# Other turns of the last tiles among three DRAM sums, and VectorE as the reporter of closed sums

## The reference

```python
x = x + tanh(g_xattn) * xattn(ctx, ctx, layernorm(x), ssm_kernel, D, 8)   # long convolution, 16 heads of 8
h = layernorm(x)                                                        # 2048 tokens x 256
s = sigmoid(h @ w_router); combine = s of the 6 chosen of 32 experts    # grouped top-k with a bias
routed = sum over the chosen e: combine[e] * (silu(h @ gate_w[e]) * (h @ up_w[e])) @ down_w[e]   # 256 -> 176 -> 256
shared = silu(h @ sh_gate_w) * (h @ sh_up_w) @ sh_down_w
out = x + tanh(g_ffn) * (routed + shared)
```

## Time and profile before

| | |
|---|---|
| median of 3 runs | 513.12 us |
| the profiled execution | 514.59 us, of which its span 512.8 us |
| PE busy | 435.5 us (85%) |
| POOL busy | 275.5 us (54%) |
| DMA at the two last slices of 40 | 9 and 9 tenths busy, 331 and 334 GB/s |
| PE clock granted there | 5 tenths of full speed; 9 or more in the slices before |

### The profile page before, as it was taken

One profiled execution on the slowest core, in us unless ns is written; L12 is line 12 of the kernel. 1 busy time (PEld: TensorE's weight loads), 2 busy tenths in 40 slices (PEclk: granted clock), 3 DMA queues, 4 the chain that ended last, 5 costly groups with the idle time before them and its releaser, 6 DMA issues.

```text
span 512.8 us, 8791 instructions
## 1 busy us (share of the span) xinstructions
PE 435.5 (85%) x2162; PEld 330.4 (64%) x2162; DVE 303.5 (59%) x1162; ACT 201.7 (39%) x522; POOL 275.5 (54%) x226
## 2 busy tenths in 40 slices
PE   0936989999999687799999999999999999999600
PEld 0726768768767565477777777777777777777400
DVE  4999898998986665334444444444444444444156
ACT  4531734644642511134444444444444444444300
POOL 2000027748758737558766666666566666666700
PEclk9986999999999698789999999999999999999955
DMA  6999913323369876858767666667666666666599
GB/s 257 383 354 396 384 40 130 130 75 107 120 214 366 299 262 201 256 195 133 127 118 127 113 114 116 118 114 125 114 112 115 116 123 119 116 115 103 67 331 334
DMA packets 59462, 91.56 MB, mean 179 GB/s; under 512 B 6797, under 2 KB 50189, under 8 KB 59149
## 3 DMA queue, kind: packets, MB, share of 16 engines
q1 hardware_dynamic: 35759, 55.07, 31.9%
q0 software_dynamic: 20160, 29.11, 31.6%
q10 hardware_dynamic: 3486, 6.73, 3.9%
HBM read 47.87 MB, written 43.02 MB: 177 GB/s over the span
## 4 chain that ended last, share of the span: by engine, by line
PE 69%; DVE 16%; DMA 7%; ACT 4%; issue 3%; DVEq 0%; SPq 0%; POOL 0%; POOLq 0%; ACTq 0%
PE bank L1261 24%; PE bank L1280 18%; PE bank L1250 5%; PE bank L1271 4%; DVE arena L702 4%; PE bank L1123 4%; PE bank L1103 3%; PE bank L1144 3%; PE bank L1091 3%; DMA arena<-token_sums 2%; DMA token_sums<-shd_sb,dest 2%; DMA payload<-expert_lists 2%; PE bank L1092 1%; ACT payload L548 1%; DVE arena L659 1%
## 5 line engine op out<-in xcount | busy, mean ns | idle before, releaser
L430 POOL DMA_INDIRECT expert_lists<-payload,slots x96 | 103.5, 1078 | 116.2 <-DVE slots L809 77.8
L1261 PE MATMUL bank<-wgu,work 128*128 x432 | 148.1, 466 | 1.3 <-DVE work L1018 1.3
L1280 PE MATMUL bank<-wd,work 88*128 x432 | 111.9, 382 | 0.0
L1036 DVE TENSOR_TENSOR work<-work,bank 128x176 f32<-128x176 f32 x108 | 36.5, 338 | 121.8 <-ACT work L593 121.8
L1261 PEld LDWEIGHTS bank<-wgu,work 128*128 128x128 f32 x432 | 74.8, 193 | 25.4 <-issue 2.9
L593 ACT ACTIVATE work<-bank 128x176 f32<-128x176 f32 x108 | 34.2, 317 | 111.4 <-PE bank L1261 111.4
L1280 PEld LDWEIGHTS bank<-wd,work 88*128 88x128 f32 x432 | 73.9, 191 | 6.2 <-issue 0.2
L445 POOL DMA_INDIRECT token_sums<-shgu_sb,dest x35 | 54.5, 1558 | 29.8 <-ACT shgu_sb L608 25.5
L1018 DVE COPY work<-bank 128x256 f32<-128x256 f32 x108 | 45.8, 424 | 28.9 <-PE bank L1250 28.9
L445 POOL DMA_INDIRECT token_sums<-q_sb,dest x28 | 43.6, 1558 | 23.6 <-ACT q_sb L608 15.9
L702 DVE TENSOR_TENSOR arena<-arena,q_sb 128x448 f32<-128x448 f32 (+7 forms) x120 | 45.4, 456 | 1.7 <-ACT arena L496 1.6
(11 more groups left out here) (174 smaller groups left out, 569.5 us busy)
## 6 DMA issues: line engine op xcount, KB each, us to landing
payload<-expert_lists SPq DMA_DIRECT2D x108, 152.0 KB, 2.6
wgu<-w_gu SPq DMA_DIRECT2D x9, 704.0 KB
expert_lists<-blank SPq DMA_DIRECT2D x1, 5016.0 KB, 23.4
wgu<-w_gu SPq DMA_DIRECT2D x1, 4928.0 KB, 18.9
arena<-token_sums SPq DMA_DIRECT2D x9, 512.0 KB, 8.8
wd<-w_down SPq DMA_DIRECT2D x4, 704.0 KB
token_sums<-blank SPq DMA_DIRECT2D x1, 2304.0 KB, 26.6
token_sums<-blank SPq DMA_DIRECT2D x1, 2176.0 KB, 23.0
```

What stands on the lines that cost most here:

```text
L430: nc.gpsimd.indirect_dma_start(lists, bass.IndirectOffsetOnAxis(ap=slots[:, g % 2, b, k:k + 1], axis=0), pay[g % 2][:, b, :], None).then_i ...
L1036: nc.vector.tensor_tensor(win(work, H_AT + t % 2 * M, [[1, M]]), win(work, SG_AT + t % 2 * M, [[1, M]]), bank[2 + t % 2][:, M:2 * M], ALU. ...
L1261: last = nc.tensor.matmul(bank[2 + t % 2][:, 0:2 * M], xT_half(t, k), wgu[:, bass.ds(e * WGU_E + k * 2 * M, 2 * M)], start=(k == 0), stop= ...
L1280: last = nc.tensor.matmul(bank[6 + t % 2][:, 0:L], hT_half(t, c), wd[:, bass.ds(e * WD_E + c * L, L)], start=(c == 0), stop=(c == 1))
```

## The change

Tiles 0 to 95 stay as they are. From tile 96 on the sum is `LAST_TURN[t % 4]`: of each block of four tiles the first goes to sum 0, the second to 1, the third to 2, the fourth to 1 again. A tile waits for the last one before it in the same sum (`before_in_sum`), which is four tiles back for sums 0 and 2 and two for sum 1. The reports of closed sums leave POOL: VectorE's ending waits for the last add of sum 0, of sum 2 and of sum 1 and raises `all_added` after each. Loads and additions go in the order 0, 2, 1, and sum 1's place in SBUF becomes the output piece.

```diff
+LAST_TURN, CLOSING = (0, 1, 2, 1), (0, 2, 1)
+        def sum_of(t):
+            return t % S if t < 4 * (SURE + 1) else LAST_TURN[t % 4]
+        def before_in_sum(t):
+            return max((u for u in range(max(0, t - 4), t) if sum_of(u) == sum_of(t)), default=None)
+        def last_in_sum(n, i):
+            return max(u for u in range(4 * n, 4 * n + 4) if sum_of(u) == i)
...
-            for i in range(S):
-                sp.wait_ge(all_added, i + 1)
+            for k, i in enumerate(CLOSING):
+                sp.wait_ge(all_added, k + 1)
...
-                if t >= S:
-                    pool.wait_ge(t_added[(t - S) % NX], nth(t - S))
+                earlier = before_in_sum(t)
+                if earlier is not None:
+                    pool.wait_ge(t_added[earlier % NX], nth(earlier))
...
             def adds_end(n):
-                for i in range(S):
-                    for u in range(4 * n, 4 * n + 4):
-                        if u % S == i:
-                            pool.wait_ge(t_added[u % NX], nth(u))
-                    pool.sem_inc(all_added, 1)
+                pool.sem_inc(held, 1)
...
-                                        tile_dump[:, t:t + 1], float(t % S * SUM_ROWS), ALU.max, ALU.add)
+                                        tile_dump[:, t:t + 1], float(sum_of(t) * SUM_ROWS), ALU.max, ALU.add)
...
             def steps_end(n):
                 times(n * 4 + 3)
+                dve.wait_ge(t_h, n * 4 + 4)
+                for i in CLOSING:
+                    u = last_in_sum(n, i)
+                    dve.wait_ge(t_added[u % NX], nth(u))
+                    dve.sem_inc(all_added, 1)
...
-            for i in range(S - 1):
+            for k, i in enumerate(CLOSING[:-1]):
                 for c, (lo, hi) in enumerate(CHUNKS):
                     dve.wait_ge(sums_in[i][c], 16)
```

More of the change, by code:

```diff
@@ L636, in _ @@
                 act.dma_start(out.rearrange("b p l -> p b l")[:, lo:hi, :],
-                              win(arena, ((S - 1) * B + lo) * L, [[L, hi - lo], [1, L]])).then_inc(out_stored, 16)
+                              win(arena, (CLOSING[-1] * B + lo) * L, [[L, hi - lo], [1, L]])).then_inc(out_stored, 16)
         @block.vector
@@ L1053, in _ @@
             more_blocks(dve, last, SURE, steps_end, steps_of_block)
-            for i in range(S - 1):
+            for k, i in enumerate(CLOSING[:-1]):
                 for c, (lo, hi) in enumerate(CHUNKS):
                     dve.wait_ge(sums_in[i][c], 16)
-                    if i:
-                        dve.wait_ge(f_added, (i - 1) * len(CHUNKS) + c + 1)
+                    if k:
+                        dve.wait_ge(f_added, (k - 1) * len(CHUNKS) + c + 1)
                     r = rows[:, lo:hi, :].rearrange("p b l -> p (b l)")
@@ L1063, in _ @@
             for c, (lo, hi) in enumerate(CHUNKS):
-                dve.wait_ge(sums_in[S - 1][c], 16)
+                dve.wait_ge(sums_in[CLOSING[-1]][c], 16)
                 dve.wait_ge(f_added, (S - 2) * len(CHUNKS) + c + 1)
-                end = win(arena, ((S - 1) * B + lo) * L, [[1, (hi - lo) * L]])
+                end = win(arena, (CLOSING[-1] * B + lo) * L, [[1, (hi - lo) * L]])
                 nc.vector.scalar_tensor_tensor(end, end, gates[:, 1:2], rows[:, lo:hi, :].rearrange("p b l -> p (b l)"),
```

## The result

The changed kernel takes 520.7 us (median of 4, 519.91 to 522.91), the kernel before 513.1: a ratio of 1.0135, 95% interval 1.0107 to 1.0162, 7.6 us slower. I had forecast 515.5 us and a range up to 518.5: the direction was right, the size was a third of what came, and the time lies outside the range. The profiled execution took 522.91 us with a span of 521.1, so 8.3 us more than the one before.

The account below looks back on a forecast made before the run. After PE's last tile, DMA engines and VectorE run nearly full; either can set the end. Earlier loads worth nothing, VectorE's gapless additions from 495.5 +2.4 us: median 513.12 to 515.5 us, range 511.9 to 518.5.

Parts of the forecast that it names:

- Sum 0 closes earlier: SP's first load of sum 0, after tile 104's landing: at 483.5 in place of 485.76, 2.25 us earlier, worth nothing in total.
- The wait on two tiles back costs nothing but 0.4 us at tile 107: Adds of tiles 99 to 107: POOL catches up at once; only tile 107's add is issued later, at 486.05, by 0.4 us.
- The early loads meet the adds: End of the adds: loads' data from 485.05 delay tiles 106 and 107, which land at 492.8 and about 494.4.
- VectorE reports, and so it waits for the last landing: VectorE's ending: no addition before tile 107's landing; additions start at 495.5 in place of 491.61, last one ends +2.4 us.
- The jump behind the report: VectorE's jump out of the If over unused blocks, formerly hidden in idle time, now exposed: 1.0 us.
- a rival with 0.08 and 2.7 us: VectorE's jump: its 8 KB code fetch is held up in full engines, 2.7 us later, time 518.2; chance 0.08.
- The sign that I had named for a dear jump: Between last landing and VectorE: idle time of over 2 us would show the jump as the larger price.
- POOL's 0.5 us as a lower bound for VectorE's jump: POOL's jump at 495.2, next instruction at 495.7: the lower of two values between which VectorE's 1.0 us was taken.
- The rule that I set beside the sum: VectorE's jump: taken branch outside the small window forces a page transfer; 1.6 us or more, total 516.1 or later.
- it wasn't stretched twice: Rival on the last adds: 106 and 107 both stretched, 107 lands at 497.5, time 518.6; chance 0.15.
- The early rival: Tile 107 lands early, before about 492.0; at 489.85 the DMA stream is the bound, 510.9; chance 0.15.

## Why the prediction was right in direction and wrong in size

- *Sum 0 closes earlier*: right. 3.7 us after tile 104's issue, forecast 3.85, before 6.1.
- *The wait on two tiles back costs nothing but 0.4 us at tile 107*: right in kind; it was 1.8 us. Tile 105 landed in 4.6 us, not 3.8, touched by the loads' first data (3.9 in the kernel that held the loads back), and from the wait to the issue 0.85 us passed, not 0.34, as POOL's branches stood in between.
- *The early loads meet the adds*: right. Tile 106 took 9.3 us to land (forecast 9.0) and tile 107 landed 15.2 us after tile 104's issue (forecast 14.75). That this came so near is in part luck: tile 107 was issued 1.35 us later than forecast and took 7.5 us in place of 8.4, and the two misses cancel but for 0.5 us.
- *VectorE reports, and so it waits for the last landing*: right. Without the jump this costs 1.2 us.
- *The jump behind the report*: **the step that failed**. I took 1.0 us between POOL's 0.5 and the 1.6 of an instruction transfer. It measured 6.2, which is 5.3 of the 5.9 us by which the profiled executions' difference (8.3) exceeds the forecast (2.4) when the 0.1 for the report is counted with it; the rest is 0.7 for tiles reached later, 0.5 for tile 107's landing, and 0.5 less for the additions, 14.8 us for 15.3. Two things were missing. The quiet jump is 2.8 us: the end of the transfer is not the end of the stall. And the transfer stands in the same full engines as the add whose 5.6 us delay I had just reckoned with. I had that as a rival with 0.08 and 2.7 us; the delay was 3.4, and its base was wrong too. The sign that I had named for a dear jump, over 2 us of idle time between the last landing and VectorE, is what came.
- *POOL's 0.5 us as a lower bound for VectorE's jump* was a poor row: POOL's next instruction there was a drain of the program's end, and nothing in the profile shows from where its code came.
- The rule that I set beside the sum, from the Trainium skill ("Runtime: NRT & Kernel Launch", section "Instruction fetch mechanics"), that a taken branch out of the fetched window stalls until the target page has been brought in by DMA, is borne out: 2.8 us with empty queues, 5.7 to 6.2 with SP's loads in them.
- *The rivals*: tile 107 didn't land early, and it wasn't stretched twice. The early rival counts on the DMA stream as the bound, which would pass the whole gain of the earlier loads on to the end. With the jump out of the way it didn't: of 2.1 us of earlier loads the tail kept 0.2 (32.9 for 33.1).

## What to carry to other kernels

A wait that is moved to an idle engine is free only if nothing of that engine's own program order needs to run before it ends: look at what stands behind the wait, and count a jump there as part of the price. Put such waits on an engine whose stream is over. And when a stream of loads is started earlier, ask which small transfers will now be queued behind it, the code's own among them.

## What the hardware showed that I had not expected

A taken jump over unused blocks costs VectorE 2.8 us with idle DMA engines (one execution) and 5.7 to 6.2 us with SP's loads at 93% of the engines or more (three executions of two kernels), and the profile puts it under "issue", with no name. In each of them exactly one instruction transfer, of 8 KB, starts between the branch and VectorE's next instruction. It starts 1.0 us behind the branch with idle engines and 3.8 to 4.4 us behind it beside the loads; from its start to VectorE's next instruction it is 1.8 to 1.9 us in all four. So only the first part of the price grows with the traffic. The jump of the kernel with the additions in the ending, beside the stores, lies between: 1.9 us to the transfer, 3.7 in all.

An indirect add issued within about half a microsecond of sum 0's first load took 7.4 to 9.5 us to land (ten executions), against a median of 3.8 in the loop. With 1 MB queued in place of 2 MB it took 6.8.
